# Flamingo cross-attention block with a routed expert layer, one Trainium2 core: rings of sixteen places for the expert results and their numbers, tile loops written out, packed expert words read later in a tile

## The reference, cut to what matters

```python
def moe(x, ew1, ew2, ew3, gate, bias):            # x: 2048 tokens x 128
    scores = sigmoid(x @ gate.T + bias)           # 9 experts
    top, selected = top_k(scores, 2)
    top = top / (sum(top) + 1e-20)
    cw = einsum('tk,tke->te', top, one_hot(selected, 9))
    out = 0
    for e in range(9):
        h = silu(x @ ew1[e].T) * (x @ ew3[e].T)   # 352 hidden
        out = out + cw[:, e:e+1] * (h @ ew2[e].T)
    return out

x = x + tanh(g_xattn) * cross_attention(ctx, layernorm(x), mask, mask)   # 16 sequences x 128, 8 heads
x = x + tanh(g_ffn) * moe(layernorm(x))
```

## Time and profile before

| | us |
|---|---|
| median of 3 runs | 225.47 |
| lowest, highest | 224.35, 226.18 |
| the profiled execution, its own time | 226.1 |
| its span, first to last instruction | 223.8 |
| of the profiled execution outside the span | 2.3 |
| TensorE busy within the span | 207.0 |
| instruction fetches in the page's table of DMA queues | 15 and 13 packets |

### The profile page before, as it was taken

One profiled execution on the slowest core, in us unless ns is written; L12 is line 12 of the kernel. 1 busy time (PEld: TensorE's weight loads), 2 busy tenths in 40 slices (PEclk: granted clock), 3 DMA queues, 4 the chain that ended last, 5 costly groups with the idle time before them and its releaser, 6 DMA issues.

```text
span 223.8 us, 5950 instructions
## 1 busy us (share of the span) xinstructions
PE 207.0 (93%) x1618; PEld 166.2 (74%) x1618; DVE 148.1 (66%) x523; ACT 142.0 (63%) x398; POOL 134.2 (60%) x246
## 2 busy tenths in 40 slices
PE   8999995999999999899889899979999997999892
PEld 3677653567666676566559698969999996999892
DVE  0459999477889679888776988334434433434963
ACT  2275869887897877678646666646666655676200
POOL 5228647024322787578678888888888876546210
PEclk9999999799999999999997999999999999999999
DMA  6999999999960000001137332223222221270293
GB/s 175 359 372 242 403 401 405 409 401 312 350 189 1 25 27 24 24 27 37 40 83 202 87 95 62 60 72 80 80 74 58 64 65 39 62 231 32 63 372 130
DMA packets 23598, 34.88 MB, mean 156 GB/s; under 512 B 2561, under 2 KB 15878, under 8 KB 23442
## 3 DMA queue, kind: packets, MB, share of 16 engines
q1 hardware_dynamic: 20610, 29.27, 39.3%
q0 software_dynamic: 2240, 4.23, 5.7%
q10 hardware_dynamic: 720, 1.02, 1.5%
HBM read 15.85 MB, written 19.06 MB: 156 GB/s over the span
## 4 chain that ended last, share of the span: by engine, by line
PE 55%; DVE 14%; POOL 14%; ACT 5%; issue 5%; DMA 5%; SPq 1%; POOLq 0%; ACTq 0%; DVEq 0%
PE pt_ps L1352 9%; POOL x_rows L591 7%; PE score_ps L1165 5%; DMA ctx_r<-in_ctxT 4%; PE score_ps L1310 4%; PE pt_ps L1361 4%; PE ps_a L1215 4%; PE score_ps L1311 3%; PE score_ps L1312 3%; POOL spare L569 3%; PE pt_ps L1203 3%; PE ps_b L1272 2%; DVE less L823 2%; ACT probs L398 2%; PE score_ps L1115 2%
## 5 line engine op out<-in xcount | busy, mean ns | idle before, releaser
L611 POOL DMA_INDIRECT y_rows<-probsT,ids x38 | 37.7, 992 | 12.7 <-ACT probsT L470 6.2
L398 ACT ACTIVATE probs<-score_ps,less 128x128 f32<-128x128 f32 x128 | 37.6, 409 | 0.4 <-DVE less L823 0.4
L591 POOL DMA_INDIRECT x_rows<-stage,slot x32 | 32.6, 1018 | 8.0 <-POOL spare L569 4.5
L1352 PE MATMUL pt_ps<-w,probsT 128*128 x234 | 33.0, 277 | 3.7 <-ACT probsT L477 3.3
L1352 PEld LDWEIGHTS pt_ps<-w,probsT 128*128 128x128 f32 x234 | 30.6, 191 | 5.2 <-issue 5.0
L470 ACT ACTIVATE probsT<-pt_ps,xg 128x128 f32<-128x128 f32 x38 | 14.0, 368 | 30.0 <-PE pt_ps L1352 21.9
L1039 DVE TENSOR_TENSOR xg_low<-ps_a,xg_high 128x128 fp32r<-128x128 f32 x40 | 11.6, 291 | 30.3 <-ACT xg_high L452 17.7
L1310 PE MATMUL score_ps<-w_high,xg_low 128*128 x80 | 29.8, 372 | 0.3
L1048 DVE TENSOR_TENSOR probs<-probs,score_ps 128x352 f32<-128x352 f32 x40 | 20.8, 521 | 10.2 <-PE score_ps L1312 3.0
L1312 PE MATMUL score_ps<-w_high,xg_high 128*128 x80 | 26.3, 329 | 0.0
L1311 PE MATMUL score_ps<-w_low,xg_high 128*128 x80 | 26.2, 327 | 0.0
(11 more groups left out here) (178 smaller groups left out, 457.0 us busy)
## 6 DMA issues: line engine op xcount, KB each, us to landing
x_rows<-pads SPq DMA_DIRECT2D x1, 9945.0 KB, 36.0
w_low<-in_w13T SPq DMA_DIRECT2D x3, 1056.0 KB, 11.6
xg<-x_rows SPq DMA_DIRECT2D x40, 65.0 KB
ctx_r<-in_ctxT SPq DMA_DIRECT2D x4, 512.0 KB, 7.5
y_rows<-pads SPq DMA_DIRECT2D x1, 2048.0 KB, 15.3
w<-in_w2T SPq DMA_DIRECT2D x1, 1728.0 KB, 9.8
kheads<-y_rows SPq DMA_DIRECT2D x3, 512.0 KB, 5.2
mask_b<-in_mask SPq DMA_DIRECT2D x4, 256.0 KB, 8.2
```

Source lines behind the costliest of these rows:

```text
L398: last = nc.scalar.activation(probs[:, r % 2, h, :], score_ps[:, r % 2, h, :], ACT.Exp, bias=less[:, r % 2, h:h + 1])
L591: pool.indirect_dma_start(x_rows[:, :], bass.IndirectOffsetOnAxis(ap=slot[:, par, c, p:p + 1], axis=0), stage[:, par, c, p, :], None, boun ...
L611: pool.indirect_dma_start(y_rows[:, :], bass.IndirectOffsetOnAxis(ap=ids[:, r:r + 1], axis=0), yt[:, r, :], None, bounds_check=last_row, o ...
L1352: last = nc.tensor.matmul(into[:, 0:D], hidT[:, q3, c, :], w2[:, bass.ds(e3, 1), c, :].rearrange("p o d -> p (o d)"), start=(c == 0), stop ...
```

## The change

Three edits go together. The rings `yt`, `ids_in` and `ids` get `YR` = 16 places, `yt` moves into the attention's `vals` buffer, which is not read in the tile stage, and GpSimd's copy now itself waits for the scatter of tile k-16 while VectorE's cast waits for GpSimd's copy of tile t-16. The loops on ScalarE, VectorE and SP are gone: all 43 steps are written out. On TensorE the packed word is read after the hidden matmuls of step k, not at its top, and the expert of tile k is split off there in every step, one step ahead of its use.

```diff
-TR = 8
+TR, YR = 8, 16
...
-        yt = flat[1][:, 2 * NC * P:2 * NC * P + TR * D].rearrange("p (r d) -> p r d", r=TR)
+        yt = vals[:].rearrange("p b h d -> p (b h d)")[:, 0:YR * D].rearrange("p (r d) -> p r d", r=YR)
...
-        def tile_turns(eng, step, between):
-            for k in range(sum(EARLY)):
+        def tile_turns(step, between):
+            for k in range(NT + 3):
                 step(k, k % TR, k // TR)
                 between(k)
-            with eng.Fori(sum(EARLY) // TR, NT // TR) as i:
-                for r in range(TR):
-                    step(i * TR + r, r, i)
-            for k in range(NT, NT + 3):
-                step(k, k % TR, k // TR)
...
-            with sp.Fori(len(EARLY), NT // TR) as i:
-                for r in range(TR):
-                    sp.wait_ge(ids_cast, i * TR + (r + 1 - TR))
-                    sp.wait_ge(y_done, i * TR + (r + 1 - TR))
-                    row = sp.value_load(row_of[0:1, bass.ds(i * TR + r, 1)], min_val=0, max_val=NE * CAP)
-                    sp.dma_start(xg[:, r, :], x_rows[bass.ds(row, P), :]).then_inc(ld_tile[r], 16)
+            for t in range(sum(EARLY), NT):
+                sp.wait_ge(ids_cast, t + 1 - TR)
+                sp.wait_ge(y_done, t + 1 - TR)
+                row = sp.value_load(row_of[0:1, t:t + 1], min_val=0, max_val=NE * CAP)
+                sp.dma_start(xg[:, t % TR, :], x_rows[bass.ds(row, P), :]).then_inc(ld_tile[t % TR], 16)
...
-            for r in range(TR):
-                sp.wait_ge(st_y[r], (NT // TR - (1 if r >= TR - SUMMED else 0)) * 16)
+            for place in range(YR):
+                sp.wait_ge(st_y[place], len(range(place, NT - SUMMED, YR)) * 16)
...
                     act.wait_ge(y_mm, t + 1)
-                    if not isinstance(k, int) or t >= TR:
-                        act.wait_ge(st_y[place], turn * 16)
+                    if t >= YR:
+                        act.wait_ge(st_y[t % YR], t // YR * 16)
...
             def tile(k, r):
+                s = k % YR
                 pool.wait_ge(ids_cast, k + 1)
+                if k >= YR:
+                    pool.wait_ge(st_y[s], k // YR * 16)
...
                 dve.wait_ge(ld_tile[place], turn * 16 + 16)
-                if not isinstance(t, int) or t >= TR:
-                    dve.wait_ge(st_y[place], turn * 16)
+                if t >= YR:
+                    dve.wait_ge(ids_copied, t + 1 - YR)
...
             def tile(k, r, i):
-                if r == 0:
-                    unpacked.clear()
                 if has(k, 0):
-                    if r % PACK == PACK - 1:
-                        if r == TR - 1 and i < len(EARLY):
-                            pe.wait_ge(table_set, i + 2)
-                        unpack_next(i, r // PACK + 1)
                     pe.wait_ge(ld_tile[r], i * 16 + 16)
...
                     hidden(bank[2 + q], q, e, 1).then_inc(h3_mm, 1)
+                if has(k, 0):
+                    if r % PACK == PACK - 1:
+                        if r == TR - 1 and i < len(EARLY):
+                            pe.wait_ge(table_set, i + 2)
+                        unpack_next(i, r // PACK + 1)
+                    expert_of(k)
```

More of the change, by code:

```diff
@@ L173, in build @@
         st_last = [sem(f"st_last{n}") for n in range(UN)]
-        st_y = [sem(f"st_y{n}") for n in range(TR)]
+        st_y = [sem(f"st_y{n}") for n in range(YR)]
         ld_y = [sem(f"ld_y{n}") for n in range(len(PARTS))]
@@ L240, in in_switch @@
         def in_switch(k):
-            return isinstance(k, int) and k == SWITCH
+            return k == SWITCH
         def is_last(t):
-            return isinstance(t, int) and t == NT - 1
+            return t == NT - 1
         @block.sync
@@ L449, in tile @@
                     act.wait_ge(x_turned, k + 1)
-                    if not isinstance(k, int) or k >= 2:
+                    if k >= 2:
                         act.wait_ge(h3_mm, k - 1)
@@ L456, in tile @@
                     act.wait_ge(h1_mm, t + 1)
-                    if not isinstance(t, int) or t >= 2:
+                    if t >= 2:
                         act.wait_ge(hid_done, t - 1)
                     nc.scalar.activation(gated[:, q, :], bank[q][:, 0:HID], ACT.Silu).then_inc(silu_done, 1)
-                if isinstance(k, int) and k == SWITCH - 1:
+                if k == SWITCH - 1:
                     turned_back(NB + 2)
@@ L483, in between @@
                     nc.scalar.preload_act_table(ACT.Silu)
-            tile_turns(act, tile, between)
+            tile_turns(tile, between)
             for u in range(BY_PE[0]):
@@ L1078, in between @@
                     pass_tiles(2)
-            tile_turns(dve, tile, between)
+            tile_turns(tile, between)
             for u in range(NB // UN):
@@ L1180, in step @@
                     pe.wait_ge(r_done, NG + 1)
-                if isinstance(k, int) and k == UN:
+                if k == UN:
                     pe.wait_ge(kh_pool, NG + 2)
@@ L1296, in unpack_next, with expert_of @@
                     pe.reg_load(late if n % 2 else early, experts_packed[0:1, bass.ds(i * 2 + n, 1)])
[L1298 to L1303, removed]
+            def expert_of(t):
+                if t not in unpacked:
+                    pack = pe.snap(early if t % TR < PACK else late, min_val=0, max_val=SHIFT ** PACK - 1)
+                    unpacked[t] = pe.snap(pack // SHIFT ** (t % PACK) % SHIFT)
+                return unpacked[t]
             def hidden(dst, q, e, a):
@@ L1331, in tile @@
                     t, q = k - 1, (r - 1) % 2
-                    e = expert(r - 1)
+                    e = expert_of(k - 1)
                     pe.wait_ge(x_low, t + 1)
-                    if not isinstance(t, int) or t >= 2:
+                    if t >= 2:
                         pe.wait_ge(hid_done, t - 1)
@@ L1341, in tile @@
                     t3, q3 = k - 3, (r - 3) % 2
-                    e3 = expert(r - 3)
+                    e3 = expert_of(k - 3)
                     into = bank[5]
@@ L1374, in between @@
                     rank(NG - 1)
-            for k in range(NT + 3):
-                tile(k, k % TR, k // TR)
-                between(k)
+            tile_turns(tile, between)
             pe.wait_ge(ranks_kept, NG)
@@ L1391, in _ @@
                     for n in range(SUMMED):
-                        last = nc.tensor.matmul(here, chosen_rows[:, n, u * UN + b, :], yt[:, TR - SUMMED + n, :], start=(n == 0 and u not in BY_PE), stop=(n == SUMMED - 1))
+                        last = nc.tensor.matmul(here, chosen_rows[:, n, u * UN + b, :], yt[:, (NT - SUMMED + n) % YR, :], start=(n == 0 and u not in BY_PE), stop=(n == SUMMED - 1))
                 last.then_inc(summed, 1)
```

31 lines of the change are left out of this document (15 added, 16 removed).

## The result

| | before | changed |
|---|---|---|
| median, us | 224.91 (223.32 to 226.18) | 219.25 (219.03 to 219.53) |
| ratio, 95% interval | | 0.976 [0.972, 0.980] |
| span of the profiled execution | 223.8 | 217.2 |
| last `w2` group in it starts at | 208.09 | 201.48 |

The forecast was 222.8 us, with a range of 220.6 to 224.9. Both medians are of four runs.

The account below looks back on a forecast made before the run. TensorE was taken to set the pace at 2.07 us a step, with losses above that. Ring 1.82 plus word 0.86 gave 2.68 us off the median 225.47: 222.8 us, range 220.6 to 224.9.

Parts of the forecast that it names:

- The ring: Sixteen places remove tile 10's wait for the scatter of tile 2: 1.82 us, bounds 0 and 1.82.
- the restart of TensorE's pipeline: Part of the second `w2` gap after the wait for tile 2's scatter: 0.11 us, counted in the ring's gain.
- The word: Packed word read behind the hidden matmuls in steps 11, 15 to 39 no longer delays them: 0.86 us, bounds 0 and 1.5.
- third gap: Late TensorE signals at 182 to 189 us: 6.00 us for two steps of 4.14, a loss of 1.86 us.
- The loops: Writing out loops removes register work and branches on ScalarE and VectorE: costed at 0, upper bound 1.86 us.
- rival 4: Slower: new code on ScalarE, VectorE and SP is fetched late; three fetches fully exposed give 227.6 us; chance 0.06.
- The waits added: GpSimd's added waits cost 0.9 us but its last scatter stays covered by 2.6 us; VectorE's and SP's are hidden.
- Rival 1: The third gap, 1.86 us near a loop return, goes with the loops: 220.9 us; chance 0.22.
- Rival 2: Only the ring gains; the moved word read delays the `w2` matmuls by as much: 223.7 us; chance 0.17.
- Rival 3: The load of tile 16 replaces the ring's wait at steps 16 to 18: 224.6 us; chance 0.05.

Follow-up runs that it names:

- set of four corners: Four kernels on one chip: ring of eight or sixteen, each with the word read early or late; 224.84, 223.70, 220.21 and 219.08 us.
- first set: First four follow-up kernels, each with only part of the change, on a chip where the kernel before took 226.72 us; 224.22 to 227.22 us.
- e8: The kernel before, unchanged, run again: 224.84 us, ratio 1.001.
- e12: The kernel before with ten matmuls into an unused bank ahead of the ring's wait in step 14: 223.49 us, ratio 0.997.
- e1: The changed kernel with both rings back at eight places: 226.55 us, ratio 0.999.
- e11: The changed kernel with rings of eight, word read late and loops written out, run again on another chip: 223.70 us, ratio 0.997.
- third set: The same four kernels as the set of four corners, run on one chip; 219.08 to 224.84 us.
- e4: The kernel before with only the word read late, loops and rings of eight kept: 227.22 us, ratio 1.002.
- e3: The changed kernel with rings of eight and the word read early, so only the loops are gone: 226.23 us, ratio 0.998.
- e7: The changed kernel with SP's loop over the last 24 loads put back: 219.63 us, ratio 0.978.
- e5: The changed kernel run again, as it is: 219.28 us, ratio 0.977.
- e13: The changed kernel with SP reading the rows of tiles 16 to 19 ahead of its waits: 218.72 us, ratio 0.974.
- e15: The changed kernel with rings of eight and ten matmuls into an unused bank in step 14: 222.72 us, ratio 0.991.
- later sets: All follow-up runs after the first set, eleven profiles; the kernel before took 224.43 to 224.84 us in them.

## Why the prediction was wrong in size

**The ring: the step that failed.** "The ring is worth 1.71 + 0.11 = 1.82 us" took the wait of one execution for the wait of the kernel; measured is 4.6 us in the set of four corners (2.0 in the first set). By the rows of e8 and e12 it is some 3.3 us of wait, where 1.82 was forecast, and 1.4 of clock, which the sum didn't have. The mechanism was right, and the two ends of the wait were read rightly: the scatter of tile 2 ends it, and ScalarE's result of tile 10 begins it. But only one of them moves with TensorE. On record the scatter was issued 31.3 us after the first turn (145.65 - 114.33), in e8 31.0; tile 10 could have gone on 31.6 us after it, in e8 30.1. What made tile 10 late on record is, by all signs, the slow stretch of TensorE's clock at 117 to 123 us, which I named at the head of the prediction and didn't connect: 31.77 us to the turn of tile 14, where the 12 profiles without such a stretch need 30.03 to 30.54 and the five with it 30.71 to 31.77. The same code up to there shows the difference: 30.28 and 30.35 us in e8 and e12. No experiment brought the stretch about or took it away. A TensorE that is 1.5 us later waits 1.3 us less for the same scatter. "Since all of the removed waits are in the order of the instructions, they should be in every run" is true of the wait and false of its size. And my upper bound, 1.82 us, was that same execution's value, no bound at all.

**The clock after the wait.** The prediction counted 0.11 us for "the restart of TensorE's pipeline". After waits as long as in e1, e8 and e11 the clock falls to 1.2 GHz for 3.4 us or more, and in e8 against e12 that costs 1.4 us; in the medians of e12 and the kernel before it is 0.9.

**The word.** 0.86 us forecast; 1.1 twice in the third set, but not clear of noise, so the term is neither confirmed nor refuted. The forecast left out step 7, whose turn came 2.46 us after step 6's and now 2.30. In the first set e4 showed nothing of it; with the third gap there, a TensorE that comes earlier may only wait longer, but that was not tried.

**The loops.** 0 forecast; e3 0.998 [0.995, 1.000], e7 against e5 0.35 us with overlapping intervals. No cost of the branch can be told from noise, in either direction. The rule that the prediction weighed there (the Trainium skill, page "Runtime: NRT & Kernel Launch", section "Instruction fetch mechanics") speaks of a target outside the two pages held; no run shows whether these loops' targets were such, so the runs don't test it. Three more instruction fetches came, as estimated for rival 4, and no step from 12 to 39 is longer for it (30.90, 4.12 and 18.95 us on record).

**The waits added** are covered, as forecast: GpSimd's last scatter still follows ScalarE's result of tile 37, which ends at 200.14, by 0.75 us; the row names GpSimd's own copy of the numbers, which ends 0.04 us later and itself follows VectorE's cast for the same tile. The tail is unchanged.

**The rivals.** Rival 1 put a time near the result (220.9 us) on the wrong cause: the gap is there without the loops and away with them. I had read it as "a thing that comes and goes", and that it is. Rival 2, that only the ring gains, isn't ruled out in its mechanism, since the word's gain isn't clear of noise; its size of the ring is wrong as the forecast's is. Rival 3 is true in small: the load of tile 16 was given 1.88 us and a margin of 0.4 to 0.7; tile 17's took 3.39 us, and 1.1 us is lost in steps 16 to 18 when TensorE comes on time. Without it the ring would have shown about a microsecond more, as e13 does.

**The sum.** 4.6 + 1.1 = 5.7 us, where 1.82 + 0.86 = 2.68 were forecast. Of the 3.0 us missed the ring has 2.8. That the two profiles on record differ within the stage by nearly as much, 5.95 us, is chance: they get there by 1.88 us of third gap, which most profiles lack, and by a ring's wait shorter than most.

Open stays one small thing. Steps take 2.06 us with rings of ten or sixteen and 2.08 with eight, also where nobody is seen to wait (29-39: 18.95 against 19.10 us in e11 and e15, whose word is late as well). And what the late signals of the third gap are was not found.

## What to carry to other kernels

A wait between two chains has the size of their distance in one execution. Before pricing its removal, ask what placed each end in this profile (here a slow stretch of the clock 25 us earlier), and place both ends by their usual times; the upper bound is the wait with the late end on time. A wait of some 3 us inside a dense stage of TensorE can cost nearly half as much again afterwards through the clock (1.4 us on 3.3 in e8), and if it can't be removed, matmuls that nobody needs, put ahead of it, can get that part back. A run's mean clock tells how often the clock fell, not where; for that a profile is needed. Once a ring is deep enough, more places bring nothing (ten did what sixteen did), and the load that comes next to it on the same scatters deserves its look.

## What the hardware showed that I had not expected

An idle time of 2.83 us in a stage that is otherwise full of matmuls was followed by 3.4 us at 1.2 GHz (e8), and ten matmuls of 512 columns, 2.33 us long, kept the clock at 2.4 GHz through the same wait (e12). A fall doesn't always follow: e4 stood idle for 2.98 us and kept its clock. The kernel before has two groups of times, 222.95 to 224.00 and 224.08 to 226.01 us, one fall of the clock apart by their mean clock. And with a fall of 3.4 us at the head of the stage the kernel before lost less at the ring (2.02 us against 4.68 in e8): TensorE came later to a wait whose end hardly moved.

In the profile on record, in e3 and in e4 the other engines saw TensorE's results more than 1 us late near 182 to 189 us, with loops and without (e3: 1.85 us). In none of the eleven profiles of the later sets did they.
